# Router logits of a graph stage in column tiles, and a bias added by TensorE in an attention stage

## The chip, the cores and the metric

The kernel runs on one core of a Trainium2 chip. The metric is device time in microseconds (us) of one execution, the median of three. The engines are named as in the profile: PE is TensorE (PEld its loads of the stationary operand), DVE is VectorE, ACT is ScalarE, POOL is GpSimd, SP is SyncE, whose queue issues most DMAs.

## The reference

Four layers are added one after another to `x` (8 graphs of 1024 nodes with 128 features); each reads a normalised `x`. All numbers are fp32.

```python
x = x + gnn0(layernorm(x), adj)     # degrees, adj @ (x theta) * norm, gate
x = x + moe(layernorm(x))           # shared FFN + top 2 of 8 experts
x = x + gnn1(layernorm(x), adj)     # attention graph layer
x = x + slicing(layernorm(x))       # slices, a scan over them, and back
```

The change touches the router of the second layer and the first linear map of the third:

```python
rw = softmax(x @ Wr)                          # Wr is 128 x 8
topw, topi = top_k(rw, 2)
...
X = heads(leaky_relu(node_feats @ W_lin + b_lin))     # 4 heads of 32
q = heads(leaky_relu(node_feats @ W_q)); k = heads(leaky_relu(node_feats @ W_k))
att = sigmoid(q @ k.T * scale)
adj_h = adj * att; deg = sum(adj_h, -1); dis = deg ** -0.5
Y = (dis[:, None] * adj_h * dis[None, :]) @ X
```

## The kernel before

The program is a row of stages. Every engine has its own instruction list, written out graph by graph in Python, and runs it in order; semaphores tie the lists together. There is no scheduler: what stands next in an engine's list waits until its semaphores are up, and all behind it waits too.

**The front stage** (`front_stage`, the first 250 us) does the first layer for graphs `i` = 0 to 7, and in the same loop turn the router for graph `r = i - 2`. A turn of the PE list is: `x_transposes(i)` (normalised `x` into the PSUM tile TP), `x2_transposes(i-2)` (the second layer's input into FG), `out_transposes(i-1)` (the aggregate of the graph before, copied to SBUF by ACT into `carry`, back through TP), `transform(i)` (three weight products per 128 nodes into DG and FG), `aggregate(i, 0)` (first 512 columns of the adjacency product, into AG), `logits(i-2)`, `degrees(i+1)` (column sums of the next adjacency, in four column tiles of 32), `aggregate(i, 1)` with `degree_transposes(i+1)` in its middle, and `rank(i-2)`. The logits of one graph are eight matmuls: a tile of 128 nodes of `x2T` is the stationary operand, the 8 router columns `Wg` move.

What PE waits for in a turn comes from DVE and ACT. DVE reads the transform (`read_transform`), finishes the graph before (`begin_finish`, `finish`), chooses two experts from the logits (`choose`, from L1001) and only then issues `make_shift` (L954), for which ACT waits with `normalise_mid` (16 activations, L850). Behind these in ACT's list stand `copy_agg(i, 1)` (L863), `copy_xnT(i+1)` (L815) and `copy_x2T`. `out_transposes(i)` on PE waits for `copy_agg(i, 1)` (its data) and for `copy_xnT(i+1)` (which frees TP).

The graphs `r` = 6 and 7 get their logits after the loop, among the first groups of the expert layer.

**The attention stage** (`attention_gnn_stage`, 636 to 1103 us) works in 16 steps for each graph: two halves of the queries by eight tiles of 128 keys. In a step, PE does `scores` (L1417, into four PSUM banks `c_S`), ACT the sigmoid of them (L1552), DVE the product with the adjacency tile (`multiply`, L1586), and PE `degrees` two steps later (L1444, `c_DG`) and `products` 18 steps later (L1430, `c_YA`). Into this, each engine's list puts side jobs by the step number `n`; PE's all go through the one PSUM bank `c_M` and are counted by `side_full` and `side_free`. PE's are in the tables `AFTER_DEGREES` and `AFTER_PRODUCTS`:

```python
AFTER_DEGREES = {0: ("k1", 0, SECOND_HALF), 1: ("q1", 0, WHOLE), 2: ("deg1", -1, WHOLE),
                 5: ("x0", 0, FIRST_HALF), 6: ("x0", 0, SECOND_HALF), 7: ("x1", 0, WHOLE),
                 ...
AFTER_PRODUCTS = {4: ("y0", -2), 5: ("y1", -2), 9: ("xn0", 1), 10: ("xn1", 1)}
```

The jobs `x0` and `x1` are `X` before the leaky ReLU, for node tiles 0 to 3 and 4 to 7 (L1477): for each tile four matmuls, one for each head, that write 32 PSUM partitions each. DVE adds the bias on the way out of PSUM (`add_bias`, L1700) at `n` = 6 and 7, and applies the leaky ReLU to all of it at `n` = 11. At those same steps ACT normalises the next graph's input (`normalise_X`, L1523, at `n` = 6, 7 and 8).

A shape such as `128*32` in a PE row is the tile of the array that a matmul uses: rows by columns. Each fp32 matmul of the code stands in the trace as two MATMUL rows, transposes as one.

## Time and profile before

| | |
|---|---|
| median of 3 runs | 1422.14 us (1418.39 to 1423.32) |
| the profiled execution | 1419.9 us, of which the span from first to last instruction is 1418.2 us |
| front loop, one turn | 28.5 us |
| attention, one graph | 55 us |
| busy over the span | PE 1337.5 us (94%), DVE 962.3 us (68%), ACT 794.9 us (56%), POOL 581.7 us (41%) |

The profile is one execution. Its own time stands 2.2 us under the median of the runs, so differences are worked out against 1419.9 us and then set on the median. A busy share says little about what bounds a stage: the rows further down show where an engine stands idle and what ended the idle time.

### The profile page before, as it was taken

The numbers are of one execution on the slowest core, as the hardware profiler recorded it, in microseconds if no ns is written. First come the engines' busy times: TensorE is split into PE (matmuls) and PEld (weight loads), VectorE is DVE, ScalarE is ACT, GpSimd is POOL, SyncE is SP. The second block draws the span as 40 slices with busy tenths as digits, with TensorE's granted clock in tenths as the row PEclk, the third lists the DMA queues.
The fourth block names the chain that finished last, engine by engine and source line by source line (L and its number), as shares of the span: only waits on it lengthen the run. The fifth ranks groups of instructions, "written<-read, shape, count | busy, mean of one in ns | idle before, by whom it ended". The sixth has DMA issues, their size and how long they took to land. (4 is left out here: it accounts for less than half of the span.)

```text
span 1418.2 us, 27578 instructions
## 1 busy us (share of the span) xinstructions
PE 1337.5 (94%) x10184; PEld 806.0 (57%) x10184; DVE 962.3 (68%) x2147; ACT 794.9 (56%) x1334; POOL 581.7 (41%) x504
## 2 busy tenths in 40 slices
PE   5999999999999999986899999999999789999798
PEld 3455555668999999862233233333332467774498
DVE  2467887643343434357989999999996799856533
ACT  2466654644444444436676776777874578873300
POOL 2026777672545555301212132131143699972300
PEclk9999999999999999999999999999999999999999
DMA  9757757355888878555424534333331421004034
GB/s 312 274 178 251 288 161 236 118 179 149 248 252 240 253 242 252 173 153 178 142 90 135 162 102 126 93 118 108 102 105 45 117 61 46 16 1 98 1 107 134
DMA packets 200152, 214.37 MB, mean 151 GB/s; under 512 B 22949, under 2 KB 156645, under 8 KB 200020
## 3 DMA queue, kind: packets, MB, share of 16 engines
q1 hardware_dynamic: 191604, 195.24, 45.2%
q0 software_dynamic: 8416, 17.38, 3.4%
q8 instruction: 81, 1.33, 0.4%
q14 instruction: 51, 0.42, 0.1%
HBM read 170.51 MB, written 42.06 MB: 150 GB/s over the span
## 5 line engine op out<-in xcount | busy, mean ns | idle before, releaser
L1552 ACT ACTIVATE c_AH<-c_S 128x2048 f32<-128x2048 f32 x128 | 240.6, 1880 | 130.1 <-PE c_S L1417 129.8
L1586 DVE TENSOR_TENSOR c_AH<-c_AH,c_A 128x2048 f32<-128x2048 f32 x128 | 291.9, 2285 | 23.7 <-ACT c_AH L1552 16.3
L875 ACT ACTIVATE a_A<-a_DG,a_A 128x256 f32<-128x256 f32 (+2 forms) x202 | 94.8, 509 | 192.8 <-PE a_DG L728 191.7
L618 POOL DMA_INDIRECT ys<-a_A,a_targets x135 | 131.2, 972 | 142.3 <-DVE a_A L1090 123.8
L1375 POOL TENSOR_TENSOR c_raw<-c_deg,c_power 128x16 f32<-128x16 f32 x16 | 58.2, 3636 | 243.6 <-DVE c_deg L1643 243.6
L592 POOL DMA_INDIRECT rows<-a_S,a_slots x128 | 131.9, 1030 | 51.5 <-issue 51.5
L1444 PE MATMUL c_DG<-c_AH,c_ones 128*32 128x512 f32 x1024 | 137.3, 608 | 7.9 <-DVE c_AH L1586 7.9
L1417 PE MATMUL c_S<-c_Q,c_K 32*128 32x512 f32 x928 | 132.3, 640 | 5.1 <-ACT c_AH L1552 3.1
L1430 PE MATMUL c_YA<-c_AH,c_XT 128*32 128x512 f32 x1024 | 131.9, 593 | 0.3 <-DVE c_XT L1653 0.3
L698 PE MATMUL a_AG<-a_A,x 128*128 128x512 f32 x256 | 114.4, 595 | 0.0
L728 PE MATMUL a_DG<-a_A 128*128 128x256 f32 (+2 forms) x356 | 100.5, 406 | 1.2 <-DMA a_A<-xT_all 1.1
L741 PE MATMUL a_AG<-a_A 128*128 128x128 f32 x800 | 96.8, 275 | 0.0
L741 PEld LDWEIGHTS a_AG<-a_A 128*128 128x128 f32 x800 | 93.6, 192 | 4.5 <-issue 3.9
L741 PE MATMUL a_TP<-a_A 128*128 128x128 f32 x792 | 95.8, 275 | 0.0
L741 PEld LDWEIGHTS a_TP<-a_A 128*128 128x128 f32 x792 | 92.4, 192 | 2.9 <-issue 2.4
L1417 PEld LDWEIGHTS c_S<-c_Q,c_K 32*128 32x128 f32 x928 | 36.3, 183 | 82.3 <-ACT c_AH L1552 64.0
L728 PE MATMUL a_FG<-a_A 128*128 128x256 f32 (+2 forms) x324 | 82.0, 376 | 0.0
L698 PEld LDWEIGHTS a_AG<-a_A,x 128*128 128x128 f32 x256 | 47.6, 191 | 58.5 <-issue 56.6
L1444 PEld LDWEIGHTS c_DG<-c_AH,c_ones 128*32 128x32 f32 x1024 | 20.4, 108 | 105.9 <-issue 80.5
L1085 DVE TENSOR_TENSOR a_targets<-a_A,a_spare_rows 128x2 uint32<-128x2 f32 (+1 forms) x75 | 12.0, 160 | 93.9 <-PE a_AG L741 48.5
L1869 POOL TENSOR_TENSOR s_SW<-s_SW,s_top 128x512 f32<-128x512 f32 x64 | 66.8, 1044 | 20.2 <-DVE s_top L2055 19.8
L875 ACT ACTIVATE a_A<-a_FG,a_A 128x256 f32<-128x256 f32 (+2 forms) x162 | 71.9, 470 | 2.1 <-PE a_FG L728 2.1
(428 smaller groups left out, 2497.7 us busy)
## 6 DMA issues: line engine op xcount, KB each, us to landing
a_A<-in_dram SPq DMA_DIRECT2D x76, 578.0 KB, 5.1
a_A<-in_dram SPq DMA_DIRECT2D x32, 1024.0 KB, 9.8
c_A<-in_dram SPq DMA_DIRECT2D x128, 256.0 KB, 2.6
a_A<-rows SPq DMA_DIRECT2D x60, 130.0 KB
G<-ys SPq DMA_DIRECT2D x10, 512.0 KB, 5.1
a_X<-in_dram SPq DMA_DIRECT2D x8, 512.0 KB, 13.4
a_R<-in_dram SPq DMA_DIRECT2D x8, 512.0 KB, 5.0
stream<-a_R SPq DMA_DIRECT2D x8, 512.0 KB, 9.7
```

Of the source, the lines that this page charges most:

```text
L592: pool.indirect_dma_start(rows, bass.IndirectOffsetOnAxis(ap=slots[:, k, T * i + t:T * i + t + 1], axis=0), S[i % 3][k][:, t, :], None, bo ...
L618: pool.indirect_dma_start(ys, bass.IndirectOffsetOnAxis(ap=targets[g % NY][:, t:t + 1], axis=0), Y[g % NY][:, t, :], None, bounds_check=ys ...
L698: mm = pe.matmul(AG[:, half(h)], F[:, t, :], adj(i)[:, t, half(h)], start=(t == 0), stop=(t == T - 1))
L728: pe.matmul(up_bank(g, f)[:, 0:n], w_of(g)[:, f * P:(f + 1) * P], xT_of(g)[:, 0:n], start=True, stop=True).then_inc(up_psum, 1)
L741: mm = pe.matmul(YB[g % 2][:, t, :], hT[g % 2][:, f, t * P:(t + 1) * P], w_of(g)[:, F_N + FT + f * D:F_N + FT + (f + 1) * D], start=(f == ...
L875: act.activation(hT[g % 2][:, f, 0:size(g)], up_bank(g, f)[:, 0:size(g)], ACT.Gelu, bias=w_of(g)[:, F_N + f:F_N + f + 1]).then_inc(h_ready, 1)
L1417: mm = pe.matmul(S[:, h, :], keys[rows, t * P:(t + 1) * P], queries[rows, :], start=True, stop=True)
L1430: mm = pe.matmul(YA[h * HD:(h + 1) * HD, half, :], XT[:, t, h * HD:(h + 1) * HD], ah[:, h, :], start=(t == 0), stop=(t == T - 1))
L1444: mm = pe.matmul(DG[h * HD:(h + 1) * HD, :], ones[:, :], ah[:, h, :], start=(t == 0), stop=(t == T - 1))
L1552: act.activation(AH[g % UNITS][:, :, :], S[:, :, :], ACT.Sigmoid, scale=HD ** -0.5).then_inc(att_ready, 1)
L1586: dve.tensor_tensor(ah[:, :, :], ah[:, :, :], A[g % ADJ_BUFS][:, :].unsqueeze(1).to_broadcast([P, HEADS, HALF]), ALU.mult).then_inc(ah_dve, 1)
L1869: pool.tensor_tensor(SW[k][:, :, :], SW[k][:, :, :], top[n % 3][:, :].unsqueeze(2).to_broadcast([P, SH, G_N]), ALU.subtract).then_inc(cent ...
```

## The change

In the front stage, six of the eight graphs (`r` = 0 to 5) get their logits another way. The router columns, now padded with zeros to 32, are the stationary operand, and 256 nodes move at a time: four matmuls, each into 32 PSUM partitions of its own (`wide_logits`, into `LT`). ACT copies the 128x256 result to SBUF (`copy_logits`), PE turns it back with two transposes (`logit_transposes`, into `L_side`), and DVE reads the logits from there with a strided pattern. The degrees of the next graph are cut into their two halves, and the transposes stand between them. In the attention stage, a matmul with one row of ones and the bias row is added to the same PSUM range for each tile and head, and ACT instead of DVE copies `c_M` out (`copy_X`).

```diff
-        Wg = sb("Wg", [P, E_N])
+        Wg = sb("Wg", [P, 32])
+        Lt = sb("Lt", [P, N // 4])
...
+        LT = FG[:, 1, 0:N // 4]
+        L_side = FG[:, 1, N // 4:N // 2]
+        L_found = L_side.rearrange("p (q c z) -> p c q z", q=2, c=4)[:, :, :, 0:E_N]
...
+            def wide_logits(r):
+                pe.wait_ge(x2T_ready, NH * r + NH)
+                pe.wait_ge(H_ready, T * min(r + 3, B))
+                for c in range(4):
+                    mm = pe.matmul(LT[32 * c:32 * c + 32, :], Wg[:, :], x2T_of(r)[:, bass.ts(c, N // 4)], start=True, stop=True)
+                mm.then_inc(Lt_psum, 1)
+
+            def logit_transposes(r):
+                pe.wait_ge(Lt_ready, r + 1)
+                for q in range(2):
+                    mm = pe.transpose(L_side[:, q * P:(q + 1) * P], Lt[:, q * P:(q + 1) * P], ident[:, :])
                 mm.then_inc(logits_psum, 1)
...
                 aggregate(i, 0)
                 if i >= 2:
-                    logits(i - 2)
+                    wide_logits(i - 2)
                 if i + 1 < B:
-                    degrees(i + 1)
+                    degrees(i + 1, range(1))
+                if i >= 2:
+                    logit_transposes(i - 2)
+                if i + 1 < B:
+                    degrees(i + 1, range(1, NH))
                 aggregate(i, 1, range(4))
...
+            def copy_logits(r):
+                act.wait_ge(Lt_psum, r + 1)
+                act.activation(Lt[:, :], LT, ACT.Copy).then_inc(Lt_ready, 1)
...
                 copy_agg(i, 0)
+                if i >= 2:
+                    copy_logits(i - 2)
...
-                link(dve.tensor_copy(Lg[:, :, :], LG))
+                if r < B - 2:
+                    link(dve.tensor_copy(Lg[:, :, :].rearrange("p (c q) e -> p c q e", q=2), L_found))
+                else:
+                    link(dve.tensor_copy(Lg[:, :, :], LG))
...
                 elif what[:-1] == "x":
+                    if i == 0:
+                        pe.wait_ge(w_loaded, 48)
                     for c in range(*part):
                         for j in range(HEADS):
                             at = (4 * half + c) * P + j * HD
-                            mm = pe.matmul(M[quad(j), c * P:(c + 1) * P], xnT[:, at:at + HD], W[:, 2, :], start=True, stop=True)
+                            pe.matmul(M[quad(j), c * P:(c + 1) * P], xnT[:, at:at + HD], W[:, 2, :], start=True, stop=False)
+                        for j in range(HEADS):
+                            mm = pe.matmul(M[quad(j), c * P:(c + 1) * P], ones[0:1, :], bias[0:1, :], start=False, stop=True)
...
+            def copy_X(i, half):
+                act.wait_ge(side_full, full[f"x{half}", i])
+                wait(act, xs_ready, 2 * i)
+                act.activation(flat(XR[:, tiles(half), :]), M[:, :], ACT.Copy).then_inc(side_free, 1)
...
+                    if n in (6, 7) and is_graph(i):
+                        copy_X(i, n - 6)
...
-            def add_bias(i, half):
...
-                    if n in (6, 7) and is_graph(i):
-                        add_bias(i, n - 6)
```

What is left out sets the new padding columns to zero on POOL and raises the counts of the semaphore `consts` by one.

PE's list in one front turn before, from the first half of the aggregate to the next `out_transposes` (L698 is `aggregate`, L664 `logits`, L679 `degrees`, the L102 rows the three kinds of transposes in TP, L669 and L670 `rank`, L637 `x2_transposes`):

```order
L698 MATMUL a_AG<-a_A,x 128x512 x8
L664 MATMUL a_FG<-a_Wg,a_x2T 128x8 x8
L679 MATMUL a_DG<-a_A,Wc 32x512 x16
L698 MATMUL a_AG<-a_A,x 128x512 x4
L102 MATMUL a_TP<-ident,a_dpart 128x128 x8
L698 MATMUL a_AG<-a_A,x 128x512 x4
L669 MATMUL a_FG<-a_both,Wc 128x64
L670 MATMUL a_FG<-a_both,Wc 128x64
L102 MATMUL a_TP<-ident,a_xn 128x128 x8
L637 MATMUL a_FG<-ident,a_S 128x128 x8
L102 MATMUL a_TP<-ident,carry 128x128 x8
```

The same engine and place with the change (L717 is now `aggregate`, L677 `wide_logits`, L698 `degrees`, L683 `logit_transposes`):

```order
L717 MATMUL a_AG<-a_A,x 128x512 x8
L677 MATMUL a_FG<-a_x2T,a_Wg 32x256 x4
L698 MATMUL a_DG<-a_A,Wc 32x512 x8
L683 MATMUL a_FG<-ident,a_Lt 128x128 x2
L698 MATMUL a_DG<-a_A,Wc 32x512 x8
L717 MATMUL a_AG<-a_A,x 128x512 x4
L102 MATMUL a_TP<-ident,a_dpart 128x128 x8
L717 MATMUL a_AG<-a_A,x 128x512 x4
```

Eight matmuls have become four, in the degrees' tile form, and two transposes have come between the halves of the degrees; all behind them stands as it was.

PE's list in attention before, at steps `n` = 6 and 7 of a graph (L1430 `products`, L1417 `scores`, L1444 `degrees`, L1477 the `x` job of the step):

```order
L1430 MATMUL c_YA<-c_AH,c_XT 32x512 x4
L1417 MATMUL c_S<-c_Q,c_K 128x512 x4
L1444 MATMUL c_DG<-c_AH,c_ones 32x512 x4
L1477 MATMUL c_M<-W,xnT 32x128 x8
L1430 MATMUL c_YA<-c_AH,c_XT 32x512 x4
L1417 MATMUL c_S<-c_Q,c_K 128x512 x4
L1444 MATMUL c_DG<-c_AH,c_ones 32x512 x4
L1477 MATMUL c_M<-W,xnT 32x128 x16
```

The same place with the change, for the step `n` = 6 (L1462 `products`, L1449 `scores`, L1476 `degrees`, L1511 the `x` matmuls, L1513 the bias matmuls):

```order
L1462 MATMUL c_YA<-c_AH,c_XT 32x512 x4
L1449 MATMUL c_S<-c_Q,c_K 128x512 x4
L1476 MATMUL c_DG<-c_AH,c_ones 32x512 x4
L1511 MATMUL c_M<-W,xnT 32x128 x4
L1513 MATMUL c_M<-c_bias,c_ones 32x128 x4
L1511 MATMUL c_M<-W,xnT 32x128 x4
L1513 MATMUL c_M<-c_bias,c_ones 32x128 x4
```

Each tile's four `x` matmuls are now followed by four bias matmuls of the same size of output, whose stationary operand is one row of 32 ones. The array tile that the program gives them is 32 rows by 32 columns; that of the `x` matmuls is 128 by 32.

ACT's list in attention with the change, at the same steps (L1593 the sigmoid, L1551 `copy_X`, L1564 `normalise_X`); before, it read the same without the two L1551 rows:

```order
L1593 ACTIVATE c_AH<-c_S 128x2048 [waits c_y_psum,c_s_psum] x4
L1551 ACTIVATE c_XR<-c_M 128x512 [waits c_xs_ready,c_side_full]
L1564 ACTIVATE x<-x,c_xshift,c_irstd 128x128 [waits c_x_kept,c_xshift_ready]
L1564 ACTIVATE x<-x,c_xshift,c_irstd 128x128 x2
L1593 ACTIVATE c_AH<-c_S 128x2048 [waits c_y_psum,c_s_psum]
L1551 ACTIVATE c_XR<-c_M 128x512 [waits c_xs_ready,c_side_full]
L1564 ACTIVATE x<-x,c_xshift,c_irstd 128x128 [waits c_x_kept,c_xshift_ready]
L1564 ACTIVATE x<-x,c_xshift,c_irstd 128x128 x2
```

The copy stands between a sigmoid and the normalising of the next graph, and waits for PE's `x` job of that step.

## Rows read from the trace of the kernel before

**Rows 1.** Windows: busy us (count) of each engine, PEclk, DMA, GB/s.

```profile
120.00:150.00 30.00, 29.89 (x137) 16.43 (x136) 24.11 (x92) 19.01 (x46) 22.83 (x21) 1.00 0.75 261
...
851.00:906.00 55.00, 55.00 (x588) 17.52 (x584) 52.35 (x68) 41.10 (x42) 15.25 (x4) 1.00 0.39 118
```

**Rows 2.** Timeline of PE in attention: start, us, line, tile, idle before.

```profile
862.71 1.04 PE L1481 MATMUL c_M<-xnT,W 128*32 128x512 f32 x8
863.56 1.04 PE L1430 MATMUL c_YA<-c_AH,c_XT 128*32 128x512 f32 x8
...
868.83 1.07 PE L1444 MATMUL c_DG<-c_AH,c_ones 128*32 128x512 f32 x8
869.72 1.04 PE L1430 MATMUL c_YA<-c_AH,c_XT 128*32 128x512 f32 x8
870.69 0.66 PE L1461 MATMUL c_M<-ident,carry 128*128 128x128 f32 x4
871.27 1.14 PE L1417 MATMUL c_S<-c_Q,c_K 32*128 32x512 f32 x8
872.34 1.07 PE L1444 MATMUL c_DG<-c_AH,c_ones 128*32 128x512 f32 x8
...
876.74 0.62 PE L1477 MATMUL c_M<-W,xnT 128*32 128x128 f32 x16
877.17 1.04 PE L1430 MATMUL c_YA<-c_AH,c_XT 128*32 128x512 f32 x8
```

**Rows 3.** Groups by line, whole span: busy us, mean ns, idle before, releaser.

```profile
L1477 PE MATMUL c_M<-W,xnT 128*32 128x128 f32 x512 | 18.8, 277 | 0.0
L1700 DVE TENSOR_TENSOR c_XR<-c_M,c_bias 128x512 f32<-128x512 f32 x16 | 11.0, 687 | 7.6 <-PE c_M L1477 7.6
L1510 ACT ACTIVATE c_K<-c_M 128x512 f32<-128x512 f32 x15 | 8.8, 588 | 0.0
```

**Rows 4.** Timeline of ACT in attention's first graph, steps 6 to 8.

```profile
662.29 1.88 ACT L1552 ACTIVATE c_AH<-c_S 128x2048 f32<-128x2048 f32 x1 [7.72 <-PE c_S L1417]
664.06 1.25 ACT L1523 ACTIVATE x<-x,c_xshift,c_irstd 128x128 f32<-128x128 f32 x3
665.42 1.88 ACT L1552 ACTIVATE c_AH<-c_S 128x2048 f32<-128x2048 f32 x1
...
668.65 1.88 ACT L1552 ACTIVATE c_AH<-c_S 128x2048 f32<-128x2048 f32 x1 [0.20 <-PE c_S L1417]
```

**Rows 5.** Timeline of PE in one front turn.

```profile
122.92 1.85 PE L664 MATMUL a_FG<-a_Wg,a_x2T 128*128 128x8 f32 x16
124.70 3.64 PE L679 MATMUL a_DG<-a_A,Wc 128*32 128x512 f32 x32
...
137.66 1.06 PE L637 MATMUL a_FG<-ident,a_S 128*128 128x128 f32 x8
138.56 1.04 PE L102 MATMUL a_TP<-ident,carry 128*128 128x128 f32 x8
```

**Rows 6.** Timeline of DVE in the same turn.

```profile
126.98 0.22 DVE L1001 COPY a_Lg<-a_FG 128x64 f32<-128x64 f32 x1
...
130.38 0.16 DVE L954 SCALAR_TENSOR_TENSOR a_shift<-a_jmean,a_jrstd 128x8 f32<-128x8 f32 x1
```

**Rows 7.** Timeline of ACT in the same turn.

```profile
126.69 0.60 ACT L828 ACTIVATE a_dpart<-a_DG 128x512 f32<-128x512 f32 x1 [2.97 <-PE a_DG L679]
...
130.58 6.26 ACT L850 ACTIVATE a_S<-a_R,a_shift,a_jrstd 128x128 f32<-128x128 f32 x16 [1.57 <-DVE a_shift L954]
...
136.84 0.57 ACT L863 ACTIVATE carry<-a_AG 128x512 f32<-128x512 f32 x1
137.32 1.06 ACT L815 ACTIVATE xnT<-a_TP 128x512 f32<-128x512 f32 x2
```

**Rows 8.** Timeline of ACT at the end of a turn without logits (`i` = 1).

```profile
80.30 1.06 ACT L815 ACTIVATE xnT<-a_TP 128x512 f32<-128x512 f32 x2
```

**Rows 9.** Timeline of PE at the same place.

```profile
81.45 1.06 PE L102 MATMUL a_TP<-ident,carry 128*128 128x128 f32 x8 [0.48 <-issue]
```

More of the change, by code:

```diff
@@ L281, in front_stage @@
         s_ready, x2T_psum, x2T_ready = sem("s_ready"), sem("x2T_psum"), sem("x2T_ready")
+        Lt_psum, Lt_ready = sem("Lt_psum"), sem("Lt_ready")
         logits_psum, both_ready, gap_ready, share_ready = sem("logits_psum"), sem("both_ready"), sem("gap_ready"), sem("share_ready")
@@ L407, in _ @@
             sp.dma_start(bias[:, :], b_t.rearrange("(a n) -> a n", a=1).to_broadcast([P, D])).then_inc(w_loaded, 16)
-            sp.dma_start(Wg[:, :], Wr).then_inc(w_loaded, 16)
+            sp.dma_start(Wg[:, 0:E_N], Wr).then_inc(w_loaded, 16)
             load_x(1)
             load_adj(1)
-            sp.wait_ge(consts, 14)
+            sp.wait_ge(consts, 15)
             for e in range(E_N):
@@ L566, in _ @@
             pool.memset(keep[:, :, :], 1.0).then_inc(consts, 1)
+            pool.memset(Wg[:, E_N:32], 0.0).then_inc(consts, 1)
             pool.iota(order_i[:, :, :], pattern=[[0, T], [-1, E_N]], base=E_N, channel_multiplier=0).then_inc(consts, 1)
@@ L576, in _ @@
             pool.iota(spare_i[:, :, :], pattern=[[G, NY], [P, RT]], base=2 * TOK, channel_multiplier=1).then_inc(consts, 1)
-            pool.wait_ge(consts, 12)
+            pool.wait_ge(consts, 13)
             pool.memset(keep[:, :, 0:1], 0.0).then_inc(consts, 1)
@@ L663, in logits @@
                 for t in range(T):
-                    mm = pe.matmul(LG[:, t, :], x2T_of(r)[:, t * P:(t + 1) * P], Wg[:, :], start=True, stop=True)
+                    mm = pe.matmul(LG[:, t, :], x2T_of(r)[:, t * P:(t + 1) * P], Wg[:, 0:E_N], start=True, stop=True)
+                mm.then_inc(logits_psum, 1)
+            def wide_logits(r):
[8 more added lines that the diff above has]
+                    mm = pe.transpose(L_side[:, q * P:(q + 1) * P], Lt[:, q * P:(q + 1) * P], ident[:, :])
                 mm.then_inc(logits_psum, 1)
@@ L670, in rank, with degrees @@
                 pe.matmul(TT, ones[:, :], both[:, :, :], start=True, stop=True).then_inc(rank_psum, 1)
-            def degrees(i):
+            def degrees(i, part=range(NH)):
                 pe.wait_ge(adj_loaded[i % 3], 64 * (i // 3 + 1))
@@ L675, in degrees @@
                     pe.wait_ge(H_ready, T * i)
-                for h in range(NH):
+                for h in part:
                     for t in range(T):
@@ L753, in _ @@
             pe.wait_ge(w_loaded, 80)
-            pe.wait_ge(consts, 14)
+            pe.wait_ge(consts, 15)
             for i in range(B):
@@ L1116, in _ @@
             dve.wait_ge(w_loaded, 80)
-            dve.wait_ge(consts, 14)
+            dve.wait_ge(consts, 15)
             dve.tensor_copy(spare_rows[:, :, :], spare_i[:, :, :])
@@ L1693, in leak_qk @@
                 leak(dst[:, cols(int(name[-1]))]).then_inc(qk_ready, 1)
-            def add_bias(i, half):
-                if i == 0:
-                    dve.wait_ge(w_loaded, 48)
-                dve.wait_ge(side_full, full[f"x{half}", i])
-                wait(dve, xs_ready, 2 * i)
-                dve.tensor_tensor(XR[:, tiles(half), :], quarter(M[:, :]), bias[:, :].unsqueeze(1).to_broadcast([P, 4, D]),
-                                  ALU.add).then_inc(side_free, 1)
             def leak_X(i):
```

## Prediction

> **What bounds the kernel now.** I read the windows first, for how much of a stage each engine is busy, then the timelines, for what begins when something else ends.
>
> In attention, one graph takes 55 us, and PE is busy in all 55.00 of them, DVE in 52.35, ACT in 41.10 [rows 1]. That PE is full and not only stretched is seen in its timeline: each row begins where the one before it leaves off, none carries an idle time, and a step comes out as the sum of its rows [rows 2]. The list of waits has no entry at all for PE between 850 and 960 us. DVE's 2.65 us of idle time are waits for others. So a microsecond added to PE's list in attention is a microsecond of the kernel, and one taken off DVE's list is nothing.
>
> In the front loop PE is nearly as full, 29.89 of 30 us, against 24.11 for DVE [rows 1]. But there a second chain is as long as PE's own. DVE issues `make_shift` at 130.38 as soon as it is through with choosing [rows 6]; ACT begins its 16 activations at 130.58, ends them at 136.84, copies the aggregate and then `xnT` until 138.38, with no idle time between [rows 7]; and PE's `out_transposes`, which wait for that last copy, begin at 138.56 [rows 5]. How soon they could begin is seen in a turn without logits: there the copy ended at 80.30 + 1.06 = 81.36, PE had stood idle for 0.48, and began at 81.45 [rows 8, 9], so 0.09 us after the copy. In the turn shown that would be 138.47. PE is ahead of this chain by no more than 0.09 us a turn.
>
> **The front part.** Removed: eight logit matmuls, which hold PE from 122.92 to 124.70, 1.78 us a graph [rows 5]. Added: four matmuls of 256 columns in four column tiles. Eight rows of 512 columns in that form take 0.85 us [rows 2], so these eight rows of 256 take 0.43. The two transposes are single passes of 128 columns; four abreast of 512 in two rounds make 0.43 for one pass of 512, so 0.11 for one of 128, 0.22 for both. And the order now changes the tile's form four times instead of twice; a change costs 0.14 (below), so 0.28. PE saves 1.78 - 0.93 = 0.85 us a graph, 5.1 us over six.
>
> What of it reaches the end is another matter. All that PE does earlier ends at `out_transposes`, and the chain that they wait for hangs on the start of the same turn: DVE reads the transform, finishes the graph before, chooses, shifts, and ACT follows. None of this is shortened. `choose` begins at 126.98, when DVE comes to it, though the logits were there at 124.70 [rows 5, 6]. The new logits come later: 122.92 + 0.14 + 0.43, half of the degrees (3.64 / 2 = 1.82), 0.14 and 0.22 make 125.7, still 1.3 before DVE asks. The ACT copy of 256 columns is bounded by nothing and by the 0.59 of a 512-column copy [rows 3]; it lies in the 2.97 us in which ACT is idle before 126.69 [rows 7], and PE asks for it only after half of the degrees, so I cost it at nothing; without that cover it would be its own 0.3 to 0.6 a graph. DVE's strided read has the same 64 elements and the 1.3 us ahead of it. So PE gains its 0.85 and waits for all but 0.09 of it at `out_transposes`: 0.09 in five turns is 0.45 us, call it **0.5 us** in all with what the last turn gives. Both ends: 0.5 and 5.1.
>
> **The attention part.** DVE loses 16 additions of 687 ns, 11.0 us [rows 3], under PE's full list: nothing. ACT gains 16 copies of about 588 ns [rows 3], 9.4 us. They stand in front of `normalise_X` and the next sigmoid, so what counts is whether that sigmoid still starts when PE has its scores. From the end of the scores in step 6: degrees 0.89, the `x` job with its bias 1.43 (worked out below), so the bank is full at 2.3; copy 0.59 and normalising 1.25 [rows 4] end at 4.2. The next scores end at 2.3 + 0.97 + 1.07 = 4.4. In step 7 it is 5.6 against 5.8. The copy is hidden by 0.2 us in both, so nothing; what goes over that would come on top.
>
> PE gains 512 MATMUL rows: eight for each of 64 tiles, just as many as the `x` matmuls have [rows 3], also 128 columns wide and four abreast. Sixteen such rows take 0.43 us (876.74 to 877.17) [rows 2], so the bias is 0.217 us a tile, 13.9 us in all. That it has one row of input is no discount: the columns that move are the same 128.
>
> The larger term is the change of form. The program puts the `x` matmuls on 128x32 tiles of the array and the bias on 32x32. What a change of form costs can be read from the steps. Eight rows of 512 columns between neighbours of their own form take 0.85 (862.71 to 863.56). `products`, followed by transposes of form 128*128, take 0.97 (869.72 to 870.69): 0.12 for leaving. `degrees`, after the 32*128 scores and before their own form, take 0.89 (868.83 to 869.72): 0.03 or 0.04 for entering. And where only the number of rows changes, from 128*128 to 32*128, four passes of 128 columns take 0.58 (870.69 to 871.27) instead of 0.43 [rows 2]. I take **0.14 us for a change**. No row shows a change from 128*32 to 32*32, so the bounds are nothing and, with the starts' rounding, 0.16. I take the price that all three readings give. The Trainium skill, in "TensorEngine Tiling (Array Packing)", Key Properties, says that changing the tiling mode, not just the tile, drains TensorE; by that rule the bias pays at each change, and the rows above agree for the forms that they show; without it the sum below would be 17.9 us less.
>
> Each tile is two changes, to the bias and back, so 0.217 + 0.28 = 0.50 us a tile and 4.0 us a graph. Seven graphs in which PE is full: 27.8 us. In the first graph there are no `products` yet, and PE and ACT take turns: sigmoids follow each other by 3.13 and 3.23 us [rows 4]. Step 5's two tiles delay the scores by 1.0. In step 6 the next sigmoid comes 2.3 + 0.59 + 1.25 + 0.1 = 4.2 us after the one before, 1.1 more than now. In step 7, PE's scores end at 3.4 on that count, degrees at 4.3, the four tiles' job (0.87 + 1.99) at 7.1, copy and normalising at 9.0, so 4.8 us between sigmoids, 1.6 more. Together **3.7 us**.
>
> **The sum.** 27.8 + 3.7 - 0.5 = +31.0 us. From the profiled execution's 1419.9 that gives 1450.9; the median of the runs stands 2.2 above it, so **1453 us**.
>
> **Rivals.**
> (a) No change of form is paid between `x` and bias, since both keep the same 32 columns of the array and only the rows differ. Then attention grows by 13.9 and the kernel to 1422.1 + 13.9 - 0.5 = 1435.5. Against it: the row that changes only the row count paid its 0.15 too.
> (b) The front's 5.1 us come through, if the ACT chain moves up in some way that the rows don't show: 1448.5. Against it: the 0.48 of idle in a turn that had no logits at all [rows 9].
> (c) The bias passes run one at a time and not four abreast, as they all use the first 32 rows of the array: 8 x 0.107 = 0.86 a tile instead of 0.217, 41 us more, 1494. Against it: the `x` rows also share all their rows and do run abreast. The Trainium skill, in "TensorE: Matmul & The Clock Gate", Part 3, The mechanism, says that a weight load overlaps a running matmul only where the row group differs; for the `x` rows, 27 ns each with their loads, the trace does not agree.
> (d) Faster: DVE sets the pace of attention, and PE's rows are full because they wait inside. Then taking 1.37 us a graph off DVE takes it off the kernel: 11.0 + 0.5 less, 1410.6. It needs PE's own list to be shorter than DVE's 52.35 us a graph. Against it: the rows add up to PE's 55, and the same rows take the same time in the first graph, where PE has gaps.
> (e) The bias is hidden whole, and the kernel stays within 0.3% (4.3 us, about what a measurement of it can tell from no change).
>
> **Chances.** My forecast 0.62; (a) 0.19; (b) 0.08; (c) 0.04; (d) 0.03; (e) 0.04. The range 1434 to 1459 takes in (a), (b) and a price of a change from nothing to 0.17, with about 0.2 left outside: (c), (d), (e) and the tails of the forecast. Its own range is 1447 to 1459. Faster 0.03, same 0.03 (part of (e) ends slower), slower 0.94.
>
> **What would show it.** Right, if in the changed profile a graph of attention takes 58.9 to 59.2 us and PE has no idle time in it, if step 7 grows by 2.0 us and steps 5 and 6 by 1.0 each, and if between an `x` row group of eight and the next there are 0.50 us more. With 56.7 us a graph it is (a). In the front, a turn should still take 28.4 to 28.5 us, and PE should now show an idle time of some 0.7 us before the `carry` transposes, ended by ACT; a turn of 27.7 is (b). I am wrong in kind if DVE's multiply or ACT's `copy_X` is what PE waits for in attention, and in size if a change of form costs less between two forms that share their columns.

## The result, and the profile after

The changed kernel takes 1454.07 us (median of 4 runs, 1453.57 to 1456.03), the kernel before 1421.59 us in the same runs: a ratio of 1.0235, 95% interval 1.0221 to 1.0250, so 32.5 us more. The span of its profiled execution is 1452.7 us against 1418.2.

Where the 34.5 us of span lie, cut at the same instructions in both profiles:

| stretch | before | after | difference |
|---|---|---|---|
| start to the first `carry` transposes | 54.6 | 54.9 | +0.3 |
| from there to the logits of `r` = 6 (front) | 196.85 | 196.35 | -0.5 |
| from there to the first sigmoid of attention | 385.5 | 386.9 | +1.5 |
| attention, first graph | 57.7 | 64.3 | +6.5 |
| attention, the next six graphs | 328.8 | 352.2 | +23.4 |
| attention, last graph, to its last sigmoid | 53.0 | 56.3 | +3.3 |
| from there to the end | 341.7 | 341.7 | 0.0 |

The windows of the changed kernel, one front turn and one graph of attention (columns as in [rows 1]):

```profile
120.00:148.50 28.50, 27.89 (x127) 14.15 (x126) 22.75 (x90) 18.15 (x45) 22.38 (x20) 1.00 0.74 259
886.00:944.85 58.85, 58.85 (x653) 18.25 (x649) 51.12 (x65) 42.30 (x45) 13.26 (x4) 1.00 0.35 100
```

A graph of attention has grown from 55 to 58.85 us, and PE is busy in all of it, as in [rows 1]. DVE's 52.35 us have become 51.12 in a longer graph: its freed time is idle time now. In the front turn PE, which was full, has 0.6 us of idle time.

PE's timeline at a step with two `x` tiles (start, us, line, tile; L1511 is `x`, L1513 the bias):

```profile
896.25 0.40 PE L1511 MATMUL c_M<-W,xnT 128*32 128x128 f32 x8
896.58 0.42 PE L1513 MATMUL c_M<-c_bias,c_ones 1*32 1x128 f32 x8
896.93 0.42 PE L1511 MATMUL c_M<-W,xnT 128*32 128x128 f32 x8
897.28 0.42 PE L1513 MATMUL c_M<-c_bias,c_ones 1*32 1x128 f32 x8
897.63 1.07 PE L1462 MATMUL c_YA<-c_AH,c_XT 128*32 128x512 f32 x8
```

From one group of eight to the next it is 0.33 to 0.35 us. Before, two such `x` groups in a row took 0.43 [rows 2]; these two tiles take 1.38 (896.25 to 897.63). So a tile costs 0.48 us more than before. The profile calls the bias's tile `1*32`, since only one row of its 32 is used.

PE's timeline in the front turn:

```profile
123.20 0.64 PE L677 MATMUL a_FG<-a_x2T,a_Wg 128*32 128x256 f32 x8
...
125.49 0.44 PE L683 MATMUL a_FG<-ident,a_Lt 128*128 128x128 f32 x2
125.86 1.92 PE L698 MATMUL a_DG<-a_A,Wc 128*32 128x512 f32 x16
127.71 3.70 PE L717 MATMUL a_AG<-a_A,x 128*128 128x512 f32 x8
...
138.67 1.07 PE L102 MATMUL a_TP<-ident,carry 128*128 128x128 f32 x8 [0.51 <-issue]
```

and ACT and DVE in the same turn:

```profile
137.51 1.06 ACT L838 ACTIVATE xnT<-a_TP 128x512 f32<-128x512 f32 x2
```

```profile
127.17 0.22 DVE L1031 COPY a_Lg<-a_FG 128x64 f32<-128x64 f32 x1
```

From the logits to the next `aggregate` it is 4.51 us instead of 5.35 (122.92 to 128.27 in the kernel before): 0.84 saved. The form change ahead of them costs 0.12 (110.18 to 123.20 since the last `carry` transposes, instead of 110.02 to 122.92), so PE saves 0.72 a turn. And it now waits 0.51 us before the `carry` transposes. The profile names no releaser for this wait ("issue"); that it is ACT's copy is read from the times: the copy ends at 138.57 and PE begins 0.10 us later, as it did 0.09 us behind the copy in [rows 8, 9]. The logits are there at 125.86, 1.3 us before DVE asks for them.

### The profile page after: what moved, and what is told of

Its sections match the earlier page's. It is cut to its first block and busy times, and to the rows that moved or that the text cites. A ratio compares the mean times of both kernels' runs of the same rounds, so it can differ in the third digit from the quotient of the medians.

```text
span 1452.7 us, 28547 instructions
## 1 busy us (share of the span) xinstructions
PE 1368.2 (94%) x10660; PEld 802.8 (55%) x10660; DVE 954.8 (66%) x2131; ACT 805.6 (55%) x1356; POOL 561.5 (39%) x505
## 5 line engine op out<-in xcount | busy, mean ns | idle before, releaser
L1593 ACT ACTIVATE c_AH<-c_S 128x2048 f32<-128x2048 f32 x128 | 240.5, 1879 | 136.0 <-PE c_S L1449 135.8
L1407 POOL TENSOR_TENSOR c_raw<-c_deg,c_power 128x16 f32<-128x16 f32 x16 | 54.0, 3375 | 297.3 <-DVE c_deg L1686 297.3
L1476 PE MATMUL c_DG<-c_AH,c_ones 128*32 128x512 f32 x1024 | 139.0, 615 | 7.5 <-DVE c_AH L1629 7.5
L1449 PE MATMUL c_S<-c_Q,c_K 32*128 32x512 f32 x928 | 132.3, 640 | 5.1 <-ACT c_AH L1593 3.1
L1462 PE MATMUL c_YA<-c_AH,c_XT 128*32 128x512 f32 x1024 | 132.4, 595 | 0.3 <-DVE c_XT L1696 0.3
L717 PE MATMUL a_AG<-a_A,x 128*128 128x512 f32 x256 | 114.5, 596 | 0.0
L1449 PEld LDWEIGHTS c_S<-c_Q,c_K 32*128 32x128 f32 x928 | 36.3, 183 | 82.3 <-ACT c_AH L1593 52.2
L717 PEld LDWEIGHTS a_AG<-a_A,x 128*128 128x128 f32 x256 | 47.7, 191 | 58.6 <-issue 56.7
L1476 PEld LDWEIGHTS c_DG<-c_AH,c_ones 128*32 128x32 f32 x1024 | 20.4, 108 | 105.9 <-issue 84.5
```

Source lines behind the costliest of these rows:

```text
L717: mm = pe.matmul(AG[:, half(h)], F[:, t, :], adj(i)[:, t, half(h)], start=(t == 0), stop=(t == T - 1))
L1449: mm = pe.matmul(S[:, h, :], keys[rows, t * P:(t + 1) * P], queries[rows, :], start=True, stop=True)
L1462: mm = pe.matmul(YA[h * HD:(h + 1) * HD, half, :], XT[:, t, h * HD:(h + 1) * HD], ah[:, h, :], start=(t == 0), stop=(t == T - 1))
L1476: mm = pe.matmul(DG[h * HD:(h + 1) * HD, :], ones[:, :], ah[:, h, :], start=(t == 0), stop=(t == T - 1))
L1593: act.activation(AH[g % UNITS][:, :, :], S[:, :, :], ACT.Sigmoid, scale=HD ** -0.5).then_inc(att_ready, 1)
```

## The experiments

All ratios are to the kernel before, run on the same chip in between; times in us.

| run | time | ratio, 95% interval |
|---|---|---|
| attention half alone (`att_alone`) | 1450.92 | 1.0221, 1.0201 to 1.0241 |
| bias matmuls ahead of all `x` (`att_grouped`) | 1438.70 | 1.0142, 1.0122 to 1.0162 |
| bias in the form of `x` (`att_same_form`) | 1434.84 | 1.0105, 1.0084 to 1.0125 |
| ACT copies, no bias (`att_copy_only`) | 1419.86 | 1.0000, 0.9986 to 1.0014 |
| bias twice (`att_twice`) | 1473.13 | 1.0367, 1.0352 to 1.0382 |
| front half alone (`front_alone`) | 1422.42 | 1.0019, 1.0010 to 1.0029 |
| the same again (`front_again`) | 1422.45 | 1.0018, 1.0010 to 1.0027 |
| front half, early shift (`front_early`) | 1419.69 | 0.9993, 0.9983 to 1.0002 |
| early shift alone (`early_alone`) | 1419.09 | 0.9992, 0.9981 to 1.0003 |
| early shift, two form changes fewer (`front_merged`) | 1418.74 | 0.9987, 0.9976 to 0.9999 |
| kernel before against itself (`before_again`) | 1419.90 | 1.0005, 0.9994 to 1.0016 |
| early shift, PE's list padded (`front_padded`) | 1414.89 | 0.9962, 0.9950 to 0.9975 |

### The attention half, and what of it costs

**The attention half alone** is the attention part of the diff, with the front stage of before. 

> The attention half of the change alone, front stage as before. My theory: the whole loss is here, 0.49 us a tile (0.217 of streaming and two changes of form) and 3.9 us for each graph in which PE is full; 1454.5 us, and a graph of attention 58.85 us. Rival, the front's half carries part of the loss or gives several us back: 1450 or less, or 1459 or more.

2.2%, some 31 us: nearly all of the loss is here, and a graph takes 58.85 us. The time itself is 3.6 us under the expected 1454.5; the front half, which costs 2.4 us (below), is not in it.

**Fewer changes of form**, the same matmuls in another order:

```diff
-for c in range(*part):
-    for j in range(HEADS): pe.matmul(M[quad(j), tile c], xnT.., W.., start=True, stop=False)
-    for j in range(HEADS): pe.matmul(M[quad(j), tile c], ones[0:1, :], bias[0:1, :], start=False, stop=True)
+for c in range(*part):
+    for j in range(HEADS): pe.matmul(M[quad(j), tile c], ones[0:1, :], bias[0:1, :], start=True, stop=True)
+for c in range(*part):
+    for j in range(HEADS): pe.matmul(M[quad(j), tile c], xnT.., W.., start=True, stop=True)
```

> Attention half alone, but in each job all the bias matmuls come first and then all the x matmuls, so the form changes twice a job (6 times a graph) and not twice a tile (16 times a graph); number, shape and columns of the matmuls are the same. The x matmuls overwrite the bias, so this leaves the bias out of X. My theory: 10 changes of 0.14 us fewer, a graph of attention 57.45 us, about 10 to 11 us less than the attention half as it is: 1444 us. Rival, the price lies in each bias matmul by itself (its one-row load or its pass): no difference, 1454.5 us and 58.85 a graph.

**The bias in the form of `x`**:

```diff
+part_of = sb("part_of", [P, HD])      # memset to 1/128
-mm = pe.matmul(M[quad(j), tile c], ones[0:1, :], bias[0:1, :], start=False, stop=True)
+mm = pe.matmul(M[quad(j), tile c], part_of[:, :], bias[:, :], start=False, stop=True)
```

> Attention half alone, with the bias matmuls in the form of the x matmuls: the stationary operand is 128 rows of 1/128 and the moving one the bias in all 128 rows, so that the sum is the bias and no form changes inside a job. They still accumulate on what the x matmuls have just written. My theory: only the 0.217 us of streaming a tile is left, a graph of attention 56.7 us, 1436 us. Rival 1, the extra lies in accumulating on columns just written: as dear as the attention half as it is, 58.85 a graph and 1454.5 us. Rival 2, a matmul with one input row is cheap and one with 128 is not: dearer than 1454.5.

How long a graph takes is read from an instruction that comes once a graph, `leak_X` on DVE: first and last start over the number of graphs between. The row of `att_grouped`, of `att_same_form`, and PE's timeline of a two-tile step of each:

```profile
L1701 DVE SCALAR_TENSOR_TENSOR c_XR<-c_XR x4: 1216/1218/1220, 851.4 to 1023.9; 128x1024 f32<-128x1024 f32 x4
```

```profile
885.49 0.64 PE L1478 MATMUL c_M<-c_bias,c_ones 1*32 1x128 f32 x16
886.06 0.64 PE L1482 MATMUL c_M<-W,xnT 128*32 128x128 f32 x16
886.52 1.04 PE L1430 MATMUL c_YA<-c_AH,c_XT 128*32 128x512 f32 x8
```

```profile
L1703 DVE SCALAR_TENSOR_TENSOR c_XR<-c_XR x4: 1216/1218/1221, 850.0 to 1020.0; 128x1024 f32<-128x1024 f32 x4
```

```profile
883.90 0.40 PE L1482 MATMUL c_M<-W,xnT 128*32 128x128 f32 x8
884.12 0.40 PE L1484 MATMUL c_M<-c_bias,c_part_of 128*32 128x128 f32 x8
...
884.77 1.04 PE L1432 MATMUL c_YA<-c_AH,c_XT 128*32 128x512 f32 x8
```

172.5 / 3 = 57.5 us a graph when grouped: 1.35 less for ten changes of form fewer, 0.135 each. 170.0 / 3 = 56.7 in one form: 2.15 less for sixteen fewer, 0.134 each, and every group of eight now follows the last by 0.215 to 0.22. Both give the same price, on two paths. The second still accumulates on columns just written, so that is not what costs; and its bias has 128 rows of input and is the cheaper one. The first had the same number of one-row matmuls, so those are not dear by themselves. (Its whole time fell by 12.2 us where 10 to 11 were expected: ten changes in seven graphs give 9.4, and the first graph gives 2.8, from 63.5 to 60.7; the clock in that graph is shown further down.)

**No bias at all**, so that only the copy moves to ACT and the addition leaves DVE:

```diff
-    for j in range(HEADS): pe.matmul(.., ones[0:1, :], bias[0:1, :], start=False, stop=True)
```

> Attention half without the bias matmuls: ACT copies the x job out, DVE adds nothing. This leaves the bias out of X. My theory: DVE's 11.0 us lie under PE's full list and ACT's copies are hidden, so nothing happens: 1421 us, within 0.3% of before, 55 us a graph. Rival 1, DVE sets the pace of attention: 1410 us. Rival 2, ACT's copy in front of the next sigmoid is exposed: 0.6 us for each of 16 copies, up to 1431 us.

```profile
L1698 DVE SCALAR_TENSOR_TENSOR c_XR<-c_XR x4: 1217/1218/1221, 841.5 to 1006.3; 128x1024 f32<-128x1024 f32 x4
```

164.8 / 3 = 54.9 us a graph, a ratio of 1.0000: in the full graphs DVE's 11 us bring nothing, and ACT's copies cost nothing. In the first graph, where ACT has next to no idle time in steps 6 and 7, the copies do show: from the sigmoid of the step to the next it is 3.41 and 3.38 us instead of 3.13 and 3.23 [rows 4], 0.43 more in all. The last graph is 0.6 shorter.

**The bias twice**: each tile's four bias matmuls stand in a loop of two. 

> Attention half alone with the four bias matmuls of each tile issued twice in a row, so this adds the bias twice. No further change of form. My theory: only their streaming is added, 0.217 us a tile, 1.7 us a graph; 60.6 us a graph of attention, 1454.5 + 14 = 1468.5 us. Rival, each group of four bias matmuls costs what the first one added, 0.49 us a tile: 62.8 us a graph, 1487 us.

Two graphs of this kernel first, then PE's timeline, then windows of PE's clock further on:

```profile
L1701 DVE SCALAR_TENSOR_TENSOR c_XR<-c_XR x3: 1218/1218/1219, 749.3 to 870.4; 128x1024 f32<-128x1024 f32 x3
```

```profile
904.73 0.64 PE L1482 MATMUL c_M<-c_bias,c_ones 1*32 1x128 f32 x16
905.29 0.43 PE L1479 MATMUL c_M<-W,xnT 128*32 128x128 f32 x8
```

```profile
900.00:917.00 17.00, 17.00 (x264) 6.71 (x260) 14.67 (x24) 9.27 (x8) 5.53 (x3) 1.00 0.22 67
917.00:922.00 5.00, 5.00 (x46) 1.38 (x44) 1.61 (x2) 2.33 (x5) 0.00 (x0) 0.66 0.17 52
```

121.1 / 2 = 60.55 us a graph, and a doubled bias group lasts 0.56 instead of 0.35: only streaming was added, as the theory has it. But the kernel came out 4.6 us over the expected 1468.5, which had been set on 1454.5; over the measured `att_alone` it is 22.2 us where 14 were expected. Part of that is a thing neither theory had: in two of the next six graphs the granted clock falls to half (1.2 GHz) for a while, here to a mean of 0.66 between 917 and 922, right behind the longest run of bias groups and with PE busy throughout. Each such graph takes 62.2 us, 1.6 more than the others. The first graph also grew more than planned, from 63.5 to 67.8 us.

### The front half

**The front half alone** is the front part of the diff, with attention of before. 

> The front half of the change alone, attention as before. My theory: PE's saving of 0.5 to 0.85 us a turn turns into a wait before the transposes of carry, 0.5 us of the kernel in all; same, 1421 us, a turn of 28.49 us instead of 28.54. Rival, the saving comes through: 5 us less, 1416.5 us, a turn of 27.7.

**An earlier shift**, on top of the front half, and by itself on the kernel before:

```diff
 # choose(r, between): in the second of its two rounds
 link(dve.tensor_reduce(best[:, :], sc[:, :, :], AX.X, ALU.max))
+if k == 1: between()              # make_shift(n2, 1, i - 1, shift2)
 link(dve.tensor_tensor(hot[k][:, :, :], ...))
```

> The front half alone, and DVE issues make_shift inside choose, ahead of its last four instructions, so that the chain of DVE and ACT which the transposes of carry wait for begins about 0.55 us earlier. My theory: now PE's saving comes through for about the 0.5 us a turn that PE stood idle; a turn of 28.0 us, 3 us less than the front half alone, about 1418 us. Rival 1, something else holds the turn (the power on POOL, the rank): 28.4 to 28.5 us a turn, same time as the front half alone. Rival 2, what choose still has to do is now late and costs: longer than the front half alone.

> The kernel before, with only make_shift moved up in the same way. My theory: PE's own list fills the turn but for 0.09 us, so nothing is gained: the turn stays at 28.45 to 28.54 us, 1421 us, at most 0.5 less. Rival, the chain of DVE and ACT alone holds the turn: 0.55 us a turn come through here too, 28.0 us a turn.

The `carry` transposes four turns apart, in `front_early`:

```profile
109.66 1.06 PE L102 MATMUL a_TP<-ident,carry 128*128 128x128 f32 x8
...
221.53 1.06 PE L102 MATMUL a_TP<-ident,carry 128*128 128x128 f32 x8
```

and in `early_alone`:

```profile
109.33 1.04 PE L102 MATMUL a_TP<-ident,carry 128*128 128x128 f32 x8
...
223.48 1.04 PE L102 MATMUL a_TP<-ident,carry 128*128 128x128 f32 x8
```

111.87 / 4 = 27.97 us a turn with both, and 114.15 / 4 = 28.54 with the early shift alone, which is the turn of before. In `front_alone` it is 28.53 (109.24 to 223.35), with PE waiting 0.46 to 0.58 us in each. So neither edit does anything to the turn by itself, and the two together take 0.56 us off each: PE's list and the chain of DVE and ACT are equally long, and both must get shorter.

**Two changes of form fewer**: the transposes stand behind all the degrees, next to the `aggregate` of their own form, and `make_shift` stands two instructions earlier in `choose` than in `front_early` (the expectation below says one).

```diff
-degrees(i + 1, range(1)); logit_transposes(i - 2); degrees(i + 1, range(1, NH))
+degrees(i + 1); logit_transposes(i - 2)
```

> The front half with make_shift moved up by one more instruction of choose, and the two transposes of the logits behind all the degrees, next to the aggregate that has their form, so that the tile's form changes twice and not four times. PE is 0.28 us a turn shorter, choose gets its logits about 0.4 us later. My theory: POOL's power, DVE's shift and ACT's list now set the turn, so PE's saving turns into idle time before the transposes of carry (0.3 us or more) and the turn stays at 27.9 to 28.0 us. Rival, PE's list sets the turn again: 27.7 us, 1.7 us less than with make_shift moved up alone.

```profile
108.92 1.06 PE L102 MATMUL a_TP<-ident,carry 128*128 128x128 f32 x8 [0.28 <-issue]
...
220.79 1.06 PE L102 MATMUL a_TP<-ident,carry 128*128 128x128 f32 x8 [0.32 <-issue]
```

and DVE's first read of the logits in that kernel:

```profile
126.42 0.23 DVE L1029 COPY a_Lg<-a_FG 128x64 f32<-128x64 f32 x1 [0.44 <-PE a_FG L683]
```

111.87 / 4 = 27.97 again, and an idle time of 0.28 to 0.33 us is back: the chain holds the turn, and what is taken off PE's list (4.28 us instead of 4.51 from the logits to the next `aggregate`) is time that PE waits. But the chain itself now hangs on PE: DVE waits 0.44 us for the logits, which come later, and so `make_shift` starts 19.84 us behind the last `carry` transposes (108.92 to 128.76), as in `front_early` (19.81), though it stands two instructions earlier in the list. The two edits cancel; what the earlier shift would bring with the logits in time was not run.

### What the front half costs behind the front stage

`front_alone` is 2.4 us slower than before, although its front is 0.4 shorter. **It was run again, and the kernel before against itself.**

> The front half alone a second time. It came out 2.4 us over the kernel before, though the front stage itself ended 0.4 us earlier in its profile; its later stages, whose code is the same, were longer in that one profile. Theory 1, those lengths differ from execution to execution by pauses and clock steps that have nothing to do with the change: the difference shrinks to 0 to 1 us here, and the later stages of this profile differ from the first. Theory 2, the change costs some 3 us behind the front stage each time: again 1.5 to 3.5 us over before, with the same stage long.

> The kernel before, unchanged, run as if it were another one: a ratio of 1 with an interval that holds 1, and a second profile whose stages behind the front tell how far unchanged code differs between executions (by theory 1 by 1 to 3 us in each of the expert stage, the first graph of attention and the last stages; by theory 2 they repeat within 0.5).

It repeats: 1.0018. In all four profiles so far with the wide logits and attention as before, the first graph of attention takes 59.1 to 59.5 us; in three profiles with the old logits 57.7, 56.7 and 56.9. The stages behind attention take 344.0 to 344.2 against 341.7, 343.4 and 343.6; but the changed kernel, with the wide logits, has 341.7 there, and `att_same_form`, with the old ones, 344.5, so the logits alone do not set that. The expert layer (from ACT's last copy of `x2T` to the first sigmoid) swings from 385.2 to 388.3 with the wide logits and from 384.3 to 387.8 with the old ones, so nothing is read from that.

In the first graph, the third multiply on DVE waits for its adjacency tile, 11.0 us after the first sigmoid with the old logits and 12.4 to 13.1 with the wide ones. (The expectation below calls it the fifth multiply; it is DVE's fifth instruction there.) These are the rows of `before_again`, of SP's issuing queue, ACT and DVE:

```profile
634.01 1.06 SPq L1336 DMA_DIRECT2D G<-ys  x2
634.36 1.88 ACT L1552 ACTIVATE c_AH<-c_S 128x2048 f32<-128x2048 f32 x1 [9.48 <-PE c_S L1417]
...
645.33 2.29 DVE L1586 TENSOR_TENSOR c_AH<-c_AH,c_A 128x2048 f32<-128x2048 f32 x1 [2.96 <-DMA c_A<-in_dram]
```

and of `front_early`, with the queue of the instruction loads in the 2.5 us from 632.0 behind them (packets, MB, share of 16 engines):

```profile
632.80 2.12 SPq L1370 DMA_DIRECT2D G<-ys  x2
633.15 1.88 ACT L1586 ACTIVATE c_AH<-c_S 128x2048 f32<-128x2048 f32 x1 [9.48 <-PE c_S L1451]
...
645.68 2.29 DVE L1620 TENSOR_TENSOR c_AH<-c_AH,c_A 128x2048 f32<-128x2048 f32 x1 [3.36 <-DMA c_A<-in_dram]
```

```profile
q8 instruction: 1, 0.02, 3.8%
```

Issuing the same two loads takes 2.12 us instead of 1.06, and an instruction load stands in the queues at that moment. In `before_again` there is none there; it lies 8.7 us before the first sigmoid, when nothing else moves. The wide logits make PE's list 65 instructions shorter, and the instruction load then comes at another place in time. In `front_merged` it comes 0.95 us behind the first sigmoid; there the two `G` loads are issued in 1.05 us, and it is the issue after them that is slow, 3.09 us where it takes 0.9 to 2.6 in the other profiles:

```profile
636.09 3.09 SPq L1346 DMA_DIRECT2D x<-sums  x1
```

The tile is late there too (12.4). **The last kernel gives the list its old length back**, with 33 transposes (66 instructions) where PE stands idle at the start:

```diff
 pe.wait_ge(consts, 2)
+for _ in range(33):
+    pe.transpose(AG[:, 0:P], ident[:, :], ident[:, :])
 pe.wait_ge(shift1, 1)
```

> The front half with make_shift moved up, and 33 more transposes of the identity at the very start of PE's list, where PE stands idle until 10.8 us. With the wide logits PE's list is 65 instructions shorter before the attention stage; in all four profiles with them a 16 KB instruction load lies at the first sigmoid of attention (0.2 us before it to 1.0 after), in all profiles with the old logits 8.7 to 8.9 us before it. The 66 instructions put it back. Theory: that load holds up the adjacency loads there, and this is what the wide logits cost behind the front stage; now the instruction load lies 8.7 us before the first sigmoid again, DVE's fifth multiply of attention starts 11.0 us after the first sigmoid and not 12.4 to 13.1, the first graph takes 57 us and not 59.1 to 59.5, and the kernel about 2 to 3 us less than without them: 1417 us, 0.2% under the kernel before. Rival: the late adjacency load has another cause in the front half; the first graph stays at 59 us and the kernel at 1419.7.

```profile
631.39 1.05 SPq L1372 DMA_DIRECT2D G<-ys  x2
631.74 1.88 ACT L1588 ACTIVATE c_AH<-c_S 128x2048 f32<-128x2048 f32 x1 [9.48 <-PE c_S L1453]
...
643.22 2.29 DVE L1622 TENSOR_TENSOR c_AH<-c_AH,c_A 128x2048 f32<-128x2048 f32 x1 [2.90 <-DMA c_A<-in_dram]
```

1414.89 us, 0.38% under the kernel before and the best of all. The instruction load is 8.9 us ahead of the first sigmoid again, SP issues the two loads in 1.05 us, and the multiply starts 11.48 us after the sigmoid: between the two kinds, as is the first graph with 58.2 us.

So the place of the load follows the length of PE's list; that is shown: it lies 8.6 to 8.9 us ahead of the first sigmoid in this kernel and in all eight profiles with a list of that length up to attention, and between 0.3 us ahead and 1.0 behind in the five with the shorter one. That the load makes the tile late is likely and not shown. Against it as the only cause: in `att_copy_only` and `att_twice`, with the load at its old place, another issue of SP is slow (`c_bias`, 2.33 and 2.82 us, in the other profiles 1.6 to 2.1) and the multiply starts 11.8 and 12.1 us after the sigmoid; in `att_alone` it is 9.9. The transposes that were added also change the start itself (the first `degrees` take 5.34 us instead of 3.64), but they win nothing there: the first `carry` transposes start at 55.08, at 54.91 in `front_early`.

The whole gain of this last kernel is not explained by the place of the load: the first graph gives 0.9 us of the 4 to 5 us that lie between `front_early` and this kernel, and in these two profiles the rest stands in the expert layer (385.2 and 383.7) and behind attention (344.1 and 342.0). What does that there stays open; no run told it apart from the swings of the expert layer.

## Why the prediction was right, and where it was not

The sum was +31.0 us and the measured difference is 32.5; the time forecast was 1453 and is 1454.07. The mechanism held where most of the loss lies, in the full graphs; the first graph and the front half were sized wrongly. Point by point:

**The bias.** 0.50 us a tile was forecast; 0.48 to 0.49 it is (58.85 - 54.94 = 3.91 us for eight tiles; the graph lies just under the 58.9 to 59.2 that were named as the sign). Its two terms hold apart as well: 0.217 of streaming (56.7 - 54.94 = 1.76 a graph, 0.22 a tile, in `att_same_form`) and 0.14 for a change of form (0.134 and 0.135 measured). So a change is paid also between two forms that share their 32 columns, and rivals (a), no price of form, and (c), passes one at a time, fell; (a) was the time of `att_same_form`, 1434.84 against its 1435.5, which has the front of before. The Trainium skill, in "TensorEngine Tiling (Array Packing)", Key Properties, says that changing the tiling mode drains TensorE. The trace agrees as far as it can show it: a change costs 0.135 us; a drain as such is not seen in it.

**DVE and ACT in attention.** Costed at nothing in the full graphs, where `att_copy_only` shows nothing either. Rivals (d) and (e) fell.

**The seven full graphs.** 27.8 forecast, 26.8 measured. The last one gains 0.6 that the sum did not have: a wait of PE for DVE near its end, 0.5 us, goes away when DVE has less to do; `att_copy_only` has the same 0.6.

**The first graph.** 3.7 forecast, 6.5 measured: this is the term that was mis-sized. Its sum took PE's rows at full clock and the adjacency tiles at their old times; against rival (d) it was even said that the same rows take the same time in the first graph. PE at step 5 before:

```profile
657.41 1.93 PE L1444 MATMUL c_DG<-c_AH,c_ones 128*32 128x512 f32 x8 [4.79 <-DVE c_AH L1586]
...
660.13 2.09 PE L1417 MATMUL c_S<-carry,c_K 32*128 32x512 f32 x8
```

and changed:

```profile
660.04 1.93 PE L1476 MATMUL c_DG<-c_AH,c_ones 128*32 128x512 f32 x8 [3.56 <-DVE c_AH L1629]
...
662.34 0.65 PE L1513 MATMUL c_M<-c_bias,c_ones 1*32 1x128 f32 x8
662.91 0.66 PE L1511 MATMUL c_M<-W,xnT 128*32 128x128 f32 x8
...
664.08 2.09 PE L1449 MATMUL c_S<-carry,c_K 32*128 32x512 f32 x8
```

The first sigmoid starts at 636.92 and 638.19. So these degrees start 20.49 us after it before and 21.85 now: 1.36 us are lost before the first bias matmul, since DVE's multiplies wait for an adjacency tile that is late, as in the kernels with the wide logits alone (the third one starts 12.38 us after the sigmoid, 11.02 before). From there to the next scores it is 2.72 and 4.04, 1.32 more for step 5 (1.0 forecast). The next two distances between sigmoids are 5.47 and 4.74 us instead of 3.13 and 3.23, 2.34 and 1.51 more (1.1 and 1.6 forecast). So the bias costs 5.2 us here and not 3.7, and the late tile 1.36.

The 1.5 us over the forecast lie where the clock is at half. The windows of the kernel before (the column behind POOL is the granted clock):

```profile
652.70:657.40 4.70, 0.00 (x0) 0.00 (x0) 4.60 (x16) 1.87 (x1) 2.09 (x1) 0.80 0.40 112
657.40:660.10 2.70, 2.69 (x24) 0.97 (x24) 2.70 (x3) 0.00 (x0) 1.46 (x1) 0.50 0.54 160
660.10:663.10 3.00, 3.00 (x21) 0.84 (x20) 1.74 (x1) 0.81 (x1) 0.00 (x0) 0.63 1.08 330
```

and of the changed one:

```profile
660.00:664.00 4.00, 3.96 (x40) 1.18 (x40) 4.00 (x3) 0.00 (x0) 1.49 (x1) 0.50 0.74 215
664.00:668.00 4.00, 4.00 (x24) 1.10 (x24) 0.47 (x1) 1.76 (x1) 0.00 (x0) 0.50 0.74 246
668.00:670.00 2.00, 2.00 (x40) 0.65 (x30) 1.78 (x1) 0.12 (x1) 0.00 (x0) 0.59 0.01 4
```

After a gap of PE the clock stood at half (1.2 GHz) before, for some 5 us of its work, and the first tiles of `x` fell into it. Now it stays at half for nearly 10 us of full work, and most groups of steps 5 and 6 run in it: a bias group of eight took 0.57 us there (662.34 to 662.91), not 0.35. Why the clock comes back later is told apart only in part. The windows from 664 to 668 us of `att_alone` and of `att_grouped`:

```profile
664.00:668.00 4.00, 4.00 (x32) 1.12 (x32) 1.65 (x1) 2.30 (x5) 0.00 (x0) 0.50 0.18 66
```

```profile
664.00:668.00 4.00, 4.00 (x84) 2.01 (x84) 2.45 (x2) 3.42 (x6) 0.00 (x0) 1.00 0.23 58
```

PE is busy in both from 656 us on. The first, with no late tile, is still at half; the second, with as many bias matmuls in ten fewer changes of form, is not. So the late tile is not needed for the longer stay. But in `front_early`, with the late tile and no bias matmul, the means over three windows of 4 us from 649 us are 0.53, 0.50 and 0.69, which makes 10 us at half against 7 in the kernel before (0.80, 0.50 and 0.63 over 4.7, 2.7 and 3.0 us), part of it while PE was idle. These are single profiles, and which of the two it is in the changed kernel stays open.

**The front.** PE's saving of 0.85 is 0.72, the logits are there at 125.86 (125.7 forecast), and the stage gained 0.5 us as forecast, since `out_transposes` wait; rival (b) fell. The 0.5 came together otherwise than in the sum: 0.24 in the five full turns, where 0.45 was forecast, and 0.25 in the last one. The idle time before `carry` was forecast at some 0.7 and shows as 0.51. The profile counts it from the modelled end of `x2_transposes`, 1.06 us after their start, where the next rows follow after 0.90 if nothing holds them [rows 5]: counted so it is 0.67 (137.10 to 138.67, less 0.90). That the front's half as a whole then *costs* 2.4 us was not in the sum at all: the term -0.5 had the right size for the stage and the wrong sign for the kernel. The 1.36 us of the late tile in the first graph are part of it. The seven graphs came out 1.0 us under the sum and the first graph 2.8 over it; that these errors partly cancel is luck, and the reason why the time came out so close.

## What to carry to other kernels

On a full TensorE, a small matmul in another tile form costs less by its columns than by the two changes around it: here 0.22 against 0.27 us a tile. Give it the form of its neighbours, with rows of 1/128 if need be, or put all of its kind in a row; and if the addition lies hidden on another engine under a full TensorE, leave it there. Where two chains of equal length meet, shortening one shows nothing: look for what the wait goes over to, and shorten that in the same step.

## What was not expected

The length of an engine's list moved the time: with 65 instructions fewer on PE, an instruction load came at the moment when SP issues the first loads of attention and an issue at that moment was slow (two loads in 2.12 us instead of 1.06), and the kernel was 0.2% slower though its front stage was shorter; with 66 instructions put back in idle time, the kernel with the early shift came from 0.9993 to 0.9962 of the kernel before. How the load and the rest of those microseconds hang together is not shown. And in `att_twice` the granted clock fell to half in graphs where PE had no idle time at all, behind sixteen-row groups of one-row matmuls (0.66 on the mean of 917 to 922 us, 1.6 us a time).
